# Two matmul groups of 408 and 256 columns against 152 and 512, in a fused float32r FFN kernel

## The reference

```python
c      = x @ W + (x @ A[idx]) @ Bm[idx]           # per tile one adapter of rank 16
base   = c @ W_base.T + b_base
probs  = softmax(c @ W_gate.T)                     # 8 experts
top 2 of probs, divided by their sum -> route_w    # zero for the other experts
h      = c @ A_e.T                                 # 8 experts x rank 16 = 128 columns
delta  = (h * route_w) @ B                         # back to 512 columns
out    = x + base + delta
```

## Time and profile before

| | |
|---|---|
| runs | 65.64, 65.45, 65.44 us; median 65.45 |
| profiled execution | span 64.2 us from its first to its last instruction; no other time of its own |
| PE | 60.7 us busy, 418 matmuls; 59.6 us of weight loads |
| VectorE, ScalarE, GpSimd | 36.7, 25.7 and 17.9 us busy |
| DMA | 8.46 MB moved |

### The profile page before, as it was taken

One profiled execution on the slowest core, in us unless ns is written; L12 is line 12 of the kernel. 1 busy time (PEld: TensorE's weight loads), 2 busy tenths in 40 slices (PEclk: granted clock), 3 DMA queues, 4 the chain that ended last, 5 costly groups with the idle time before them and its releaser, 6 DMA issues.

```text
span 64.2 us, 1268 instructions
## 1 busy us (share of the span) xinstructions
PE 60.7 (95%) x418; PEld 59.6 (93%) x418; DVE 36.7 (57%) x131; ACT 25.7 (40%) x73; POOL 17.9 (28%) x41
## 2 busy tenths in 40 slices
PE   4979999999999999999999999999999999999950
PEld 4969999999999999999999999999999999999940
DVE  0948599915799747020788748990477240467120
ACT  1752899507294270001163436611272011173620
POOL 1000899899988802030020301230000000000000
DMA  0799999702988102232332323800017000008044
GB/s 0 209 328 308 367 406 411 278 3 48 323 295 309 31 0 42 61 70 60 70 70 57 63 66 65 309 31 5 0 48 278 0 10 0 0 28 299 0 163 163
DMA packets 5048, 8.46 MB, mean 132 GB/s; under 512 B 1057, under 2 KB 1569, under 8 KB 5042
## 3 DMA queue, kind: packets, MB, share of 16 engines
q1 hardware_dynamic: 4370, 7.57, 36.6%
q0 software_dynamic: 384, 0.56, 2.4%
q10 hardware_dynamic: 288, 0.27, 1.2%
HBM read 5.26 MB, written 2.10 MB: 115 GB/s over the span
## 4 chain that ended last, share of the span: by engine, by line
PE 90%; DMA 5%; ACT 1%; issue 0%
PE bank L487 22%; PE bank L489 22%; PE bank L488 22%; PE bank L495 8%; PE bank L497 6%; DMA w_raw<-fold_in 5%; PE bank L573 2%; PE bank L538 2%; PE bank L554 2%; PE bank L544 2%; PE bank L577 1%; PE bank L528 1%; ACT y_out L333 1%; PE bank L584 1%; PE bank L588 1%
## 5 line engine op out<-in xcount | busy, mean ns | idle before, releaser
L487 PE MATMUL bank<-cl_hi,x_hi 128*128 128x408 f32 x32 | 11.4, 356 | 0.0
L489 PE MATMUL bank<-cl_hi,x_lo 128*128 128x408 f32 x32 | 11.2, 349 | 0.0
L488 PE MATMUL bank<-cl_lo,x_hi 128*128 128x408 f32 x32 | 11.1, 348 | 0.0
L487 PE MATMUL bank<-cr_hi,x_hi 128*128 128x256 f32 x32 | 9.6, 301 | 0.0
L489 PE MATMUL bank<-cr_hi,x_lo 128*128 128x256 f32 x32 | 9.0, 282 | 0.0
L488 PE MATMUL bank<-cr_lo,x_hi 128*128 128x256 f32 x32 | 9.0, 282 | 0.0
L261 POOL CAST cl_hi<-lora_raw 128x64 fp32r<-128x64 f32 x8 | 1.9, 239 | 16.8 <-PE bank L489 16.8
L448 DVE MAX8 top_val<-bank 128x8 f32<-128x8 f32 x8 | 1.4, 169 | 8.7 <-PE bank L538 8.7
L487 PEld LDWEIGHTS bank<-cr_hi,x_hi 128*128 128x128 f32 x32 | 6.1, 190 | 0.2
L228 POOL DMA_DIRECT2D lora_raw<-lora x8 | 4.5, 564 | 6.2 <-issue 6.1
L487 PEld LDWEIGHTS bank<-cl_hi,x_hi 128*128 128x128 f32 x32 | 6.0, 188 | 0.1
(11 more groups left out here) (99 smaller groups left out, 149.3 us busy)
## 6 DMA issues: line engine op xcount, KB each, us to landing
x_raw<-x_t SPq DMA_DIRECT2D x8, 256.0 KB, 4.5
out<-y_out SPq DMA_DIRECT2D x7, 256.0 KB, 2.1
w_raw<-fold_in SPq DMA_DIRECT2D x4, 256.0 KB, 5.1
w_raw<-fold_in SPq DMA_DIRECT2D x3, 324.0 KB, 5.2
bw_rows<-bw_hi SPq DMA_DIRECT2D x16, 40.5 KB, 2.0
lora_raw<-lora POOLq DMA_DIRECT2D x8, 64.0 KB, 3.9
bw_rows<-bw_lo SPq DMA_DIRECT2D x8, 40.5 KB, 2.1
ffn_b_raw<-ffn_b SPq DMA_DIRECT2D x1, 256.0 KB, 6.1
```

Of the source, the lines that this page charges most:

```text
L487: nc.tensor.matmul(out, a_hi, b_hi, start=first, stop=False, skip_group_check=True)
L488: nc.tensor.matmul(out, a_hi, b_lo, start=False, stop=False, skip_group_check=True)
L489: return nc.tensor.matmul(out, a_lo, b_hi, start=False, stop=last, skip_group_check=True)
```

## The change

The 664 columns by which a tile is multiplied are divided anew. `Gates(t)` takes the 16 adapter, 8 gate and 128 h columns, 152, into a bank of its own (two banks, by the parity of t). `Y(t)` takes all 512 output columns in one matmul into one bank (four banks in turn). Adapter and expert products are divided accordingly: 136 + 512 columns for the adapter's part and 512 for the experts'. Tile 7 keeps two halves of 256 output columns. The folding of the weights stays as it was; what is read out of its banks goes to cg (gate) and cy (output). The order on PE is rewritten, and with it those on ScalarE and VectorE.

```diff
-OWN = R + LEFT
+OWN = R + GH
-        left_bank = bank[0:3] + bank[7:8]
-        right_bank = bank[4:6]
+        gate_bank = bank[0:2]
+        y_bank = [bank[2], bank[4], bank[5], bank[7]]
...
-                nc.scalar.copy(cl_hi[:, i, LORA_LEFT], bank[i][:, 0:LEFT]).then_inc(cl_hi_done, 1)
+                nc.scalar.copy(cg_hi[:, i, LORA_GATE], bank[i][:, 0:GH]).then_inc(cg_hi_done, 1)
+                nc.scalar.copy(cy_hi[:, i, 0:HALF], bank[i][:, GH:LEFT]).then_inc(cl_hi_done, 1)
...
+            def copy_y(t):
+                act.wait_ge(z_done, t + 1)
+                nc.scalar.copy(y_out[:, t], y(t)[:]).then_inc(y_done, 1)
+
+            for q in range(PAIRS - 1):
                 t = 2 * q
                 copy_xa_t(q)
                 if q >= 1:
-                    copy_left(t - 2)
+                    copy_y(t - 1)
                 exp_top(t)
...
                 split_hw(t + 1)
+                copy_y(t)
+            q, t = PAIRS - 1, NT - 2
+            copy_xa_t(q)
+            exp_top(t)
+            exp_top(t + 1)
+            split_hw(t)
+            split_hw(t + 1)
+            copy_y(t - 1)
+            copy_y(t)
+            act.wait_ge(last_right_done, 1)
...
             for t in range(0, NT, 2):
                 gate(t)
                 gate(t + 1)
+                split_hw(t)
                 if t + 2 < NT:
                     split_xa(t + 2)
-                split_hw(t)
...
+            def Gates(t):
+                pe.wait_ge(x_lo_done, t + 1)
+                pe.wait_ge(la_lo_done, t + 1)
...
+                if t >= 2:
+                    pe.wait_ge(hw_done, t - 1)
+                for c in range(KC):
...
+                    mm = product(gates(t)[:, own_cols(t)], x_hi[:, t, c, :], x_lo[:, t, c, :],
+                                 cg_hi[:, c, own_cols(t)], cg_lo[:, c, own_cols(t)], c == 0, False)
+                mm.then_inc(g_done, 1)
+
+            def Y(t, chunks):
...
                 if t >= 4:
-                    pe.wait_ge(yl_done, t - 3)
+                    pe.wait_ge(y_done, t - 3)
                 for c in chunks:
...
+                    product(y(t)[:], x_hi[:, t, c, :], x_lo[:, t, c, :], cy_hi[:, c, :], cy_lo[:, c, :], c == 0, False)
...
+            Gates(0)
+            Gates(1)
+            Y(0, ALL)
+            for q in range(PAIRS - 1):
                 t = 2 * q
+                Y(t + 1, (0, 1))
                 T1(q)
+                Y(t + 1, (2, 3))
+                Lora_gates(q)
+                Y(t + 2, ALL)
+                T2(t)
+                Lora_y(t)
+                if q < PAIRS - 2:
+                    Lora_y(t + 1)
+                Gates(t + 2)
+                T2(t + 1)
+                if q < PAIRS - 2:
+                    Delta(t)
+                    Gates(t + 3)
+                    Delta(t + 1)
             t = NT - 2
+            Gates(t + 1)
+            Delta(t - 2)
+            T1(PAIRS - 1)
+            Last_left((0, 1))
+            Lora_gates(PAIRS - 1)
+            Last_left((2, 3))
+            Last_right((0,))
+            Lora_y(t - 1)
+            Lora_y(t)
             T2(t)
+            Last_right((1, 2))
+            Delta(t - 1)
             T2(t + 1)
+            Last_right((3,))
             Delta(t)
+            adapter(last_left, t + 1, slice(GH, LEFT))
+            adapter(last_right, t + 1, slice(LEFT, WIDE))
+            pe.wait_ge(hw_lo_done, NT)
+            experts(last_left, t + 1, slice(0, HALF)).then_inc(last_left_done, 1)
+            experts(last_right, t + 1, slice(HALF, D)).then_inc(last_right_done, 1)
```

More of the change, by code:

```diff
@@ L70, in adaln_ffn_kernel @@
         bias_lo = sb("bias_lo", [1, D], F32R)
[L74 to L77, removed]
+        cg_hi = sb("cg_hi", [P, KC, OWN + R], F32R)
+        cg_lo = sb("cg_lo", [P, KC, OWN + R], F32R)
+        cy_hi = sb("cy_hi", [P, KC, D], F32R)
+        cy_lo = sb("cy_lo", [P, KC, D], F32R)
         bw_hi = sb("bw_hi", [P, WIDE], F32R)
@@ L164, in a_cols, with gates, y, both @@
             return slice(0, R) if t % 2 == 0 else slice(OWN, OWN + R)
[L166 to L170, removed]
+        def gates(t):
+            return gate_bank[t % 2]
+        def y(t):
+            return y_bank[t % 4]
+        last_left, last_right = y_bank[(NT - 1) % 4][:, 0:HALF], y_bank[0][:, 0:HALF]
         def fold_right(i):
             return bank[4 + i // 2][:, i % 2 * HALF:(i % 2 + 1) * HALF]
+        def both(fold_bank):
+            return fold_bank[:].rearrange("p (c n) -> p c n", c=2)
         GATE = slice(R, R + E)
         H = slice(R + E, R + GH)
-        OUT_LEFT = slice(R + GH, OWN)
-        LORA_LEFT = slice(R, OWN)
+        LORA_GATE = slice(R, R + GH)
         def sync_program(sp):
@@ L259, in gpsimd_program @@
                 if t >= 2:
-                    pool.wait_ge(left_done, t - 1)
-                nc.gpsimd.tensor_copy(cl_hi[:, :, a_cols(t)], raw_la(t)).then_inc(la_hi_done, 1)
+                    pool.wait_ge(g_done, t - 1)
+                nc.gpsimd.tensor_copy(cg_hi[:, :, a_cols(t)], raw_la(t)).then_inc(la_hi_done, 1)
                 pool.wait_ge(la_hi_done, t + 1)
-                nc.gpsimd.tensor_tensor(cl_lo[:, :, a_cols(t)], raw_la(t), cl_hi[:, :, a_cols(t)].bitcast(F32),
+                nc.gpsimd.tensor_tensor(cg_lo[:, :, a_cols(t)], raw_la(t), cg_hi[:, :, a_cols(t)].bitcast(F32),
                                         ALU.subtract).then_inc(la_lo_done, 1)
@@ L302, in scalar_program @@
                     act.wait_ge(cr_plus_i, 1)
-                nc.scalar.copy(cr_hi[:, 2 * n:2 * n + 2, :].rearrange("p c n -> p (c n)"), bank[4 + n][:]).then_inc(cr_hi_done, 1)
+                nc.scalar.copy(cy_hi[:, 2 * n:2 * n + 2, HALF:], both(bank[4 + n])).then_inc(cr_hi_done, 1)
             split_x(2)
@@ L323, in split_hw @@
                 if t >= 2:
-                    act.wait_ge(zr_done, t - 1)
+                    act.wait_ge(z_done, t - 1)
                 nc.scalar.copy(hw_hi[:, t % 2, :], t2_bank[:, 0:P]).then_inc(hw_hi_done, 1)
[L327 to L335, removed]
+            def copy_y(t):
+                act.wait_ge(z_done, t + 1)
+                nc.scalar.copy(y_out[:, t], y(t)[:]).then_inc(y_done, 1)
+            for q in range(PAIRS - 1):
                 t = 2 * q
@@ L387, in split_left @@
             def split_left(i):
+                dve.wait_ge(cg_hi_done, i + 1)
                 dve.wait_ge(cl_hi_done, i + 1)
-                lo(cl_lo[:, i, LORA_LEFT], bank[i][:, 0:LEFT], cl_hi[:, i, LORA_LEFT], cl_lo_done)
+                lo(cg_lo[:, i, LORA_GATE], bank[i][:, 0:GH], cg_hi[:, i, LORA_GATE], cg_lo_done)
+                lo(cy_lo[:, i, 0:HALF], bank[i][:, GH:LEFT], cy_hi[:, i, 0:HALF], cl_lo_done)
             def split_right(n):
                 dve.wait_ge(cr_hi_done, n + 1)
-                lo(cr_lo[:, 2 * n:2 * n + 2, :].rearrange("p c n -> p (c n)"), bank[4 + n][:],
-                   cr_hi[:, 2 * n:2 * n + 2, :].rearrange("p c n -> p (c n)"), cr_lo_done)
+                lo(cy_lo[:, 2 * n:2 * n + 2, HALF:], both(bank[4 + n]), cy_hi[:, 2 * n:2 * n + 2, HALF:], cr_lo_done)
             dve.wait_ge(ident_ready, 1)
@@ L426, in split_xa @@
                 q = t // 2
-                dve.wait_ge(left_done, t + 1)
+                dve.wait_ge(g_done, t + 1)
                 if q >= 2:
                     dve.wait_ge(t1_done, q - 1)
-                xa = left(t)[:, a_cols(t)].unsqueeze(1).broadcast_to([P, 2, R])
+                xa = gates(t)[:, a_cols(t)].unsqueeze(1).broadcast_to([P, 2, R])
                 at = t % 2 * Q
@@ L444, in gate @@
                 n = t % 2
-                logits = left(t)[:, GATE]
-                h = left(t)[:, H].rearrange("p (e r) -> p e r", e=E)
+                logits = gates(t)[:, GATE]
+                h = gates(t)[:, H].rearrange("p (e r) -> p e r", e=E)
                 dve.wait_ge(lg_done, t // 2 + 1)
@@ L508, in Left @@
[L508 to L515, removed]
-                for c in chunks:
-                    if t == 0:
-                        pe.wait_ge(cr_lo_done, c // 2 + 1)
-                    product(right(t), x_hi[:, t, c, :], x_lo[:, t, c, :], cr_hi[:, c, :], cr_lo[:, c, :], c == 0, False)
+                    product(y(t)[:], x_hi[:, t, c, :], x_lo[:, t, c, :], cy_hi[:, c, :], cy_lo[:, c, :], c == 0, False)
@@ new lines, in Last, with Last_left, Last_right @@
+            def Last(out, cols, first_free, chunks):
+                pe.wait_ge(y_done, first_free)
+                for c in chunks:
+                    product(out, x_hi[:, NT - 1, c, :], x_lo[:, NT - 1, c, :], cy_hi[:, c, cols], cy_lo[:, c, cols],
+                            c == 0, False)
+            def Last_left(chunks):
+                pe.wait_ge(x_lo_done, NT)
+                Last(last_left, slice(0, HALF), NT - 4, chunks)
+            def Last_right(chunks):
+                Last(last_right, slice(HALF, D), NT - 3, chunks)
@@ L528, in T1, with adapter, Lora_gates @@
```

(12 more changed lines are left out.)

64 lines of the change are left out of this document (25 added, 39 removed).

## The result

The change makes the kernel slower: 70.1 us (median of four, 69.81 to 70.68) against 65.55 (65.44 to 67.03), a ratio of 1.066 with a 95% interval from 1.057 to 1.075. The forecast was 70.2. Times here are medians of all executions of a kernel; the ratios leave out those that took over 1.5% longer than that kernel's fastest.

The account below looks back on a forecast made before the run. The prediction took the tensor engine's summed matmul prices to bound the kernel. Span 64.2 plus 3.9 us of prices and 0.9 of waits gave 69.0, plus 1.25 from span to time made 70.2 us; range 65.9 to 73.0.

Parts of the forecast that it names:

- 152 columns: Price of each narrow matmul of Gates: 0.110 us, taken from the 128-column transposes, with ends 0.073 and 0.261.
- 512 columns: Price of each wide output matmul: 0.2329 us, from the straight line through the prices of 256 and 408 columns.
- x products: The 24 matmuls per tile on x: +0.445 us for each of seven tiles, +0.51 for tile 7, together +3.63.
- adapter rows: Adapter matmuls of each tile: 0.343 us after (tile 7: 0.348) for 0.30 before, together +0.35 us.
- expert products: Three matmuls of 512 columns in place of six of 256 in seven tiles: -0.08 us.
- waits at the end: PE waits before Lora_gates(3) 0.36, T2(6) 0.42, T2(7) 0.45: together 1.2 us, less 0.3 lost before, net +0.9.
- The floor: Every narrow matmul costs at least 0.110 us, set by loading 128 weight columns; chance 57%, own range 69.2 to 71.4.
- No floor: Rival: weight loads hide behind narrow matmuls too, 0.073 us each, giving 66.4 us; chance 18%.
- Plain price: Rival: narrow float32r matmuls run as plain float32, 0.261 us each, giving 85.9 us; chance 12%.
- two cycles a column: Rival: narrow matmuls take one pass at two cycles a column, 0.131 us each, giving 72.4 us; chance 6%.
- Faster: Rival: 512 columns at 0.216 us and narrow matmuls without floor, giving 64.5 us; chance 7%.
- store of tile 6: Its start only some 0.6 us before the last halves: costed at nothing, with up to 0.4 us for queueing.

Follow-up runs that it names:

- e1: Changed kernel with the 96 matmuls of Gates given only 64 of 128 weight columns: 66.32 us, ratio to before 1.014.
- e10: Changed kernel with the 96 matmuls of Gates given only 96 of 128 weight columns: 67.59 us, ratio to before 1.034.
- e2: Changed kernel with the matmuls of Gates streaming 80 columns in place of 152: 70.11 us.
- e3: Kernel before, order and banks kept, each 408-column matmul of Left split into 152 and 256 columns: 69.88 us, ratio 1.057.
- e5: Changed kernel with ScalarE's copy_y(4) moved from before copy_xa_t(3) to right behind it: 69.74 us, ratio to before 1.067.
- e9: Changed kernel with copy_y(4) behind copy_xa_t(3) and the last chunk of Last_right moved ahead of T2(7): 69.71 us, ratio to before 1.063.
- e7: Kernel before with the 96 matmuls of Right (256 columns) given only 64 of 128 weight columns: 65.34 us, ratio 0.993.
- e8: Changed kernel with the 96 matmuls of Gates given 64 of 128 feature rows per chunk, all 128 weight columns kept: 73.35 us.
- e4: Changed kernel with the matmuls of Gates widened from 152 to 256 streamed columns: 71.02 us.
- e6: Changed kernel with the 12 matmuls of Gates(1) and the 12 of Y(0) issued in turn, narrow and wide: 70.28 us.

## Why the prediction was right

By its own steps (us):

| term | forecast | measured |
|---|---|---|
| 152 columns | 0.110 | 0.1113 |
| 512 columns | 0.2329 | 0.230 |
| x products | +3.63 | 12 x 0.1113 + 12 x 0.230 = 4.096 a tile, 3.67 before; tile 7 4.20: +3.51 |
| adapter rows | +0.35 | 0.341 a tile for 0.30: +0.33 |
| expert products | -0.08 | 0.69 a tile for 0.71: -0.14 |
| waits at the end | +1.2 - 0.3 | 0.28 + 0.42 + 0.34 - 0.3 = +0.7 |
| sum | +4.8 | +4.4 by these terms, +4.33 in the stretch |

- *The floor.* The transposes were read rightly: a matmul behind a 128-column one that starts early and lasts longer waits for its weights. e1, e10 and e2 show that the load of the weight columns sets 0.11, and e3 that the floor costs 4.14 without the new order.
- *Its rivals.* "No floor" is what e1 makes true, and its forecast of 66.4 was e1's time (66.32). Plain price and two cycles a column fall with the spacing of 0.11. "Faster" asked for 512 columns below 0.2244 and narrow ones at 0.073; both failed. The formula of the Trainium skill for the gap of a warm matmul (page "TensorE: Matmul & The Clock Gate", section "Back-to-back issue gap"), which would have given 63.7, fails in the same two places: 0.111 for its 0.066, 0.230 for its 0.216.
- *512 columns.* They cost 1.2% less than the line; 112 of them make 0.3 us, the largest error of the sum. The floor, 0.0013 above the forecast for 104 matmuls, takes back 0.1.
- *The waits.* All three came where they were forecast and none in the middle, 1.04 for 1.2 in all. e5 and e9 recover 0.26 and another 0.32 in the stretch by undoing two of them, so the mechanisms are shown for these; T2(6) was not tried alone. The kernel before loses 0.12 more than the forecast took off: from 36.08 to 36.43 it does a transpose and one matmul of 256 columns, 0.23. With that the terms come to +4.3.
- *Around the stretch.* The span grew by 5.3, not 4.8. The x products began 0.7 later, by the plain float32 matmuls of the first fold, which the change doesn't touch (22.3 in e1, e5 and e9); the end came 0.27 later after the last matmul (69.5 - 66.70 against 64.2 - 61.67), inside the 0.4 kept for the store of tile 6. The last two stores take 2.0 to landing in the page of after, and 1.7 and 1.8 in that of before, the first two lines:

```profile
out<-y_out SPq DMA_DIRECT2D x1, 128.0 KB, 1.7
out<-y_out ACTq DMA_DIRECT2D x1, 128.0 KB, 1.8
...
out<-y_out SPq DMA_DIRECT2D x1, 128.0 KB, 2.0
out<-y_out ACTq DMA_DIRECT2D x1, 128.0 KB, 2.0
```

In e9, where tiles 5 and 6 are copied back to back, it is 2.1 and 2.2. That fits queueing behind the stores ahead, which was argued and not tried by itself.

- *Luck.* The time came within 0.1 of the forecast, closer than the terms: the sum was 0.5 too high, and the later end and the first fold, which differs from run to run, made up for it.

## What to carry to other kernels

Where every matmul brings new weights, price it as the larger of its stream and the load of its weight columns (here 0.11 us for 128, 0.085 for 96), so divide streamed columns such that no piece falls below the corner: by estimate about 240 columns here, where the line through 256 and 408 meets 0.111 (238 with 0.119 for 256 columns, 246 with the 0.116 of e7). Below it columns are free both ways, and interleaving with wide matmuls doesn't bring the time back. The price can be read before any change, from a short matmul such as a transpose and the lengthened row behind it.

## What was not expected of the hardware

- Matmuls of 64 rows among matmuls of 128 rows cost time at each change between them: 0.09 us at the last matmul ahead of it (e8: 26.10 to 26.30 for 152 columns, and 23.26 to 23.47 for the 256 ahead of the first) and some more at the first behind it. There are 14 changes; at 61.24, behind the last, e8 stands 37.77 us from its first matmul on x, after at the same matmul 35.49 (58.81 - 23.32). That makes 2.28, 0.16 a change, and the other run, 72.32, is just 2.2 above after. The remaining 1.3 of the 3.6 us by which the profiled stretch is longer go with the clock: the granted clock stood at 0.50, the lower of its two levels (1.2 of 2.4 GHz), from about 61.2 (the 0.81 below is a mean of both levels) to past 64, and 256 columns then took 0.21. PE had been busy without a gap from 58 on, as the windows show; why the clock fell, and why a change of rows costs time, isn't settled. The windows of e8 (columns as in the first ones above):

```profile
58.00:60.00 2.00, 2.00 (x16) 1.80 (x16) 0.82 (x4) 0.28 (x2) 0.00 (x0) 1.00 0.00 0
60.00:62.00 2.00, 2.00 (x14) 1.82 (x14) 0.66 (x3) 0.12 (x1) 0.00 (x0) 0.81 0.00 0
62.00:63.00 1.00, 1.00 (x5) 0.69 (x4) 0.00 (x0) 0.07 (x1) 0.00 (x0) 0.50 0.00 0
63.00:64.00 1.00, 1.00 (x7) 1.00 (x7) 0.00 (x0) 0.68 (x2) 0.00 (x0) 0.50 0.00 0
```

- The plain float32 matmuls of the first fold stood 0.23 apart in the profile of after and 0.12 in that of e9 while the clock column showed 1.00 in both. Eight records of after, then of e9:

```profile
3.89 2.18 PE L599 MATMUL bank<-w_raw 128*128 128x136 f32 x8 [0.28 <-DMA w_raw<-fold_in]
...
3.85 1.35 PE L601 MATMUL bank<-w_raw 128*128 128x136 f32 x8 [0.24 <-DMA w_raw<-fold_in]
```

The column can't settle it, as it shows 1.00 also where a trace has no record of the clock, and that of after has none. The traces of e4, e6, e8 and e10 have records that begin, at the full clock, only at 5.43, 5.32, 6.61 and 4.47 us, and in each the wide spacing ends within the interval between two starts in which the record begins; in e1, e5 and e9 they begin at 3.6 to 4.2, and all the spacings of the fold but the first are the narrow ones. So the slow ones ran at the lower level. PE had done 24 warm-up matmuls from 0.90 to 3.62 in all of them; why the clock rises sooner in some the runs don't say, and it moves the time of any one run by about 1 us.
